# Four expert tiles of the MoE layer moved ahead of the final table, beside the last group's attention and router

## The reference

```python
h = tok(x)                                # softmax-weighted pairs: 256 -> 128 tokens each
h = h + rwkv_attn(layernorm(h))           # a linear recurrence along the tokens
h = h + ffn(layernorm(h))                 # 192 -> 768 -> 192, exact gelu
h = h + attn(layernorm(h))                # 12 heads, softmax over the queries, + its residual
# mixture of experts on flat = h, 8192 tokens, 8 experts, the top 2 of each token:
for e in range(8):
    w_e = sum(top_w * (top_i == e))       # the token's weight for expert e, 0 for most
    out = out + w_e * (gelu(flat @ w1[e] + b1[e]) @ w2[e] + b2[e])
return h + out
```

## Time and profile before

| | |
|---|---|
| median of 3 runs | 1794.03 us |
| the profiled execution | 1808.08 us, of it the span 1806.3 us |
| busy in the span | PE 1576.6 us (87%), DVE 1369.8 (76%), ACT 1192.0 (66%), POOL 739.9 (41%) |
| mean granted clock of TensorE | 0.912 of full |
| DMA | 145.41 MB, mean 81 GB/s |

### The profile page before, as it was taken

The page is one execution under the profiler, slowest core; times in us unless marked ns, Lnnn a source line. Parts: engine busy times, 40 slices in busy tenths (PEclk is TensorE's granted clock), DMA queues, the critical chain, the costliest instruction groups (busy, mean ns, idle before and its releaser), DMA issues.

```text
span 1806.3 us, 33908 instructions
## 1 busy us (share of the span) xinstructions
PE 1576.6 (87%) x10985; PEld 1269.9 (70%) x10985; DVE 1369.8 (76%) x2810; ACT 1192.0 (66%) x3269; POOL 739.9 (41%) x743
## 2 busy tenths in 40 slices
PE   3578999999999999999999887763999999999976
PEld 2255677677677677677677666543999999999876
DVE  4675788778788788778778743334899989999986
ACT  1245787877887787778778767543666666666643
POOL 0111142332332333333233232203577777777775
PEclk6798899989999899989989978656999999999988
DMA  4000010110110111011010000244677776677662
GB/s 118 26 27 17 20 51 28 43 51 26 41 50 31 36 50 38 30 50 44 24 50 30 22 34 25 99 148 146 168 169 167 172 160 159 160 166 171 159 152 64
DMA packets 121870, 145.41 MB, mean 81 GB/s; under 512 B 21074, under 2 KB 100419, under 8 KB 121795
## 3 DMA queue, kind: packets, MB, share of 16 engines
q1 hardware_dynamic: 92432, 113.00, 20.8%
q0 software_dynamic: 26592, 29.92, 8.9%
...
## 4 chain that ended last, share of the span: by engine, by line
PE 74%; DVE 9%; ACT 8%; issue 4%; SPq 2%; POOL 1%; DMA 1%; POOLq 0%; ACTq 0%; DVEq 0%
PE ps L934 12%; PE ps L947 9%; PE ps L716 7%; PE ps L791 5%; PE ps L702 5%; PE ps L949 4%; PE ps L807 4%; PE ps L597 3%; PE ps L708 3%; PE ps L556 3%; PE ps L737 3%; PE ps L820 2%; PE ps L749 2%; ACT probs L1091 2%; PE ps L603 2%
## 5 line engine op out<-in xcount | busy, mean ns | idle before, releaser
L1330 POOL DMA_INDIRECT out<-ey,etoken x142 | 253.9, 1788 | 143.6 <-DVE ey L1847 48.4
L1091 ACT ACTIVATE probs<-ps,nmax 128x128 f32<-128x128 f32 x768 | 272.2, 397 | 24.2 <-DVE nmax L1570 24.1
L947 PE MATMUL ps<-w_hl,h_hi 128*128 128x384 f32 x852 | 252.3, 366 | 12.3 <-DVE ey L1847 12.3
L1203 ACT ACTIVATE h_full<-ps,eb 128x512 f32<-128x512 f32 (+1 forms) x234 | 158.4, 677 | 154.0 <-PE ps L934 153.8
L1570 DVE TENSOR_REDUCE nmax<-ps 128x6 f32<-128x768 f32 x128 | 121.5, 953 | 134.1 <-PE ps L791 133.0
L949 PE MATMUL ps<-w_hl,h_lo 128*128 128x192 f32 x852 | 215.4, 253 | 0.0
L1091 ACT ACTIVATION_READ_ACCUMULATOR probs<-ps,nmax 128x1 f32 x768 | 182.1, 237 | 0.0
L1320 POOL TENSOR_TENSOR w_lo<-w_raw,w_hi 128x1536 fp32r<-128x1536 f32 x39 | 156.5, 4013 | 39.4 <-ACT w_hi L1183 39.4
L947 PEld LDWEIGHTS ps<-w_hl,h_hi 128*128 128x128 f32 x852 | 162.8, 191 | 13.7 <-issue 13.2
L949 PEld LDWEIGHTS ps<-w_hl,h_lo 128*128 128x128 f32 x852 | 165.3, 194 | 0.0
L1807 DVE TENSOR_TENSOR h_lo<-h_full,h_hi 128x512 fp32r<-128x512 f32 (+1 forms) x234 | 148.0, 686 | 16.7 <-ACT h_hi L1204 16.3
...
## 6 DMA issues: line engine op xcount, KB each, us to landing
...
ex<-expert_rows_in SPq DMA_DIRECT2D x32, 528.0 KB, 5.4
...
w_raw<-in_L_ffn_w SPq DMA_DIRECT2D x78, 192.0 KB, 5.7
...
expert_rows_in<-xt SPq DMA_DIRECT2D x17, 528.0 KB, 7.0
...
```

Source lines behind the costliest of these rows:

```text
L947: nc.tensor.matmul(ps[:, 4 + s, 0:2 * C], h_hi[b][:, m, q], w2_hl[b][:, m, :], start=(m == 0), stop=False)
L1091: last = nc.scalar.activation(probs[:, t % 2, HJ * c + j, :], ps[:, 4 + j, c * P:(c + 1) * P], ACT.Exp, bias=nmax[:, t, j, c:c + 1], accum ...
L1203: nc.scalar.activation(h_full[:, m, 0:n], ps[:, m % 4, 0:n], ACT.Gelu, bias=eb1[u][:, m:m + 1])
L1330: nc.gpsimd.indirect_dma_start(total, bass.IndirectOffsetOnAxis(ap=etoken[u][:, s:s + 1], axis=0), ey[b][:, s, :], None, bounds_check=NB * ...
```

## The change

The kernel after does the first four expert tiles (`EARLY = 4`) before the final table exists.

- When 15 of the 16 groups are counted, `first_tiles` (VectorE, right after `pad_rows`) finds the expert with the most tokens and the one with the second most. Tiles 0, 1 and 2 are the first three of the former, tile 3 is the first of the latter. It writes their entries of the table and sets `first_ready`.
- SP issues, behind the pad stores, the loads of tile 0 and tile 1, the rows of tiles 2 and 3, and the weights of tile 3. Tile 2 uses tile 0's weights, which stay in their buffer, so there is one load and one split fewer of w1 and of w2 (`splits`, `kept`).
- In round 18 the steps of tiles 0 and 1 stand between those of the last group's attention and router, on each engine. Tile 0's downward half, tile 2's and tile 3's steps stand around the final table.
- The final table has NU = 35 entries, of which NFU = 28 full; it takes away from the counts what the four tiles have taken, and adds to the row of an expert's tiles the rows that are done (`begun`). It has links for that (37 in all with those of `first_tiles`, 30 before).
- SP waits for the table and the last scatter only ahead of tile 4's rows.
- `e_down` waits for the second link of the previous result (`d_exp`), not for the last (`e_y`).
- Buffers are declared in another order, so that the first tiles' buffers lie over parts of the tower that are no longer used by then; the table's temporaries move from `hid` and `buf` to `probs`.
- The helpers of the expert steps are moved ahead of `round_` unchanged, but for the bank that tile 0's transposes use (`rows_bank`: 0, later 2) and the ranges of blocks that `e_gelu` and `e_low` take.

```diff
+    EARLY = 4
+    NFU, NU = NF - EARLY, NT - EARLY
...
+            kept = 1 if t[1] % HB == 0 and at_least(t, HB) else 0
+            return (LB // HB) * t[0] + t[1] // HB + 1 - kept
+
+        def splits(t, d=0):
+
+
+            n = number(t) + d
+            return n if not isinstance(t[0], int) or n >= HB else n + 1
 
         def at_least(t, n):
             return not isinstance(t[0], int) or number(t) >= n
+
+        def last_round(i):
+            return isinstance(i, int) and i == NG + 2
+
+        def early(j):
+
+
+            return (j // LB, j % LB)
+
+        def rows_bank(t):
+
+
+            return 2 if at_least(t, 1) else 0
...
-            sp.wait_ge(S["h_stored"], 16 * NG)
-            sp.wait_ge(S["scattered"], 16 * 2 * G * NG)
-            sp.wait_ge(S["table_ready"], 1)
...
-                    if not at_least(t, 1):
-                        load_weights(t)
-                        sp.wait_ge(S["pads_stored"], 16 * (2 * E + 1))
-                        load_rows(t)
...
+            sp.wait_ge(S["first_ready"], 1)
             sp.wait_ge(S["b1_stored"], 16)
-            expert_steps(sp, e_step, 0)
+            load_weights(early(0))
+            sp.wait_ge(S["scattered"], 16 * 2 * G * (NG - 1))
+            load_rows(early(0))
+            load_rows(early(1))
+            load_weights(early(1))
+            load_rows(early(2))
+            load_rows(early(3))
+            load_biases(early(2))
+            store_h(NG - 1)
+            load_weights(early(3))
+
+
+            sp.wait_ge(S["pads_stored"], 16 * (2 * E + 1))
+            sp.wait_ge(S["scattered"], 16 * 2 * G * NG)
+            sp.wait_ge(S["table_ready"], 1)
+            expert_steps(sp, e_step, EARLY)
...
+                    if m == 3 and not at_least(t, 1):
+                        pe.wait_ge(S["hF_ready"], G * NG)
...
+                if at_least(t, 1):
+                    pe.wait_ge(S["d_exp"], RESULT_LINKS * j)
+                else:
+                    pe.wait_ge(S["counted"], 1)
...
                 if gr is not None: c_project(gr, 1)
+                if last_round(i): e_transposes(early(0))
                 if gr is not None: c_values(gr, 2, gc)
...
+                if last_round(i): e_up(early(0))
                 if gr is not None: r_transposes(gr, gc)
+                if last_round(i): e_transposes(early(1))
...
                 if gb is not None: b_mlp_up(gb, 3)
+                if last_round(i): e_up(early(1))
                 if gr is not None: r_places(gr)
...
+            e_transposes(early(2))
             pe.wait_ge(S["slots_ready"], NG)
             counts(NG)
...
+            e_down(early(0))
...
-            expert_steps(pe, e_step, -2)
+            expert_steps(pe, e_step, 1)
...
                 if gr is not None: c_exps(gr, 1, 1)
+                if last_round(i): e_weights(early(0))
                 if gc is not None: ln_out(gc, "c", hnC, hC, rstdC, shiftC)
...
                 if gr is not None: c_values(gr, 1)
+                if last_round(i): e_weights(early(1))
                 if ga is not None: a_kv(ga, "k", k_s)
                 if gr is not None: c_exps(gr, 3, 0)
                 if gr is not None: c_exps(gr, 3, 1)
                 if gr is not None: c_values(gr, 2)
+                if last_round(i): e_rows(early(0))
                 if gc is not None: transposed(gc, "c", hTC, 4)
...
                 if gb is not None: transposed(gb, "b", hTB, 2)
+                if last_round(i): e_gelu(early(0), (0, 1))
                 if gr is not None: r_out(gr)
+                if last_round(i): e_gelu(early(0), (2, 3))
                 if gr is not None: transposed(gr, "r", hTC, 4)
+                if last_round(i): e_rows(early(1))
+                if last_round(i): e_gelu(early(0), (4, 5))
...
+            e_gelu(early(1))
+            e_rows(early(2))
+            e_weights(early(3))
+            e_gelu(early(2))
+            e_rows(early(3))
+            e_gelu(early(3))
+            e_weights(early(4))
+            e_rows(early(4))
...
-            expert_steps(act, e_step, -2)
+            expert_steps(act, e_step, 3)
...
+                if gs is not None: r_scatter(gs)
+                if last_round(i): e_weights(early(0))
+                if last_round(i): e_weights(early(1))
+
+            rounds(pool, round_)
...
-            pool.wait_ge(S["pads_stored"], 16 * (2 * E + 1))
-            expert_steps(pool, e_step, -2)
+            pool.wait_ge(S["h_stored"], 16 * NG)
+            expert_steps(pool, e_step, 1)
...
+            def first_tiles():
...
+                link = table.link
+                link(nc.vector.max(most_n[:, :], n_seen[:, :]))
+                link(nc.vector.max_index(most_i[:, :], most_n[:, :], n_seen[:, :]))
+                link(nc.vector.tensor_copy(most[:, :], most_i[:, 0:2]))
+                nc.vector.tensor_copy(expert_of[:, 0:3], most[:, 0:1].to_broadcast([P, 3]))
+                nc.vector.tensor_copy(expert_of[:, 3:4], most[:, 1:2])
+                nc.vector.tensor_scalar(most_off[:, 0:3], tile_i[0:1, 0:3], float(ET), None, ALU.mult)
+                nc.vector.memset(most_off[:, 3:4], 0.0)
+                nc.vector.tensor_tensor(taken[:, 0, :], lane8[:, 0, :], most[:, 0:1].to_broadcast([P, E]), ALU.is_equal)
+                link(nc.vector.tensor_tensor(taken[:, 1, :], lane8[:, 0, :], most[:, 1:2].to_broadcast([P, E]),
+                                             ALU.is_equal))
+                link(nc.vector.scalar_tensor_tensor(taken[:, 0, :], taken[:, 0, :], 3.0, taken[:, 1, :], ALU.mult, ALU.add))
+                nc.vector.tensor_copy(unit[:, :], tile_i[:, :])
+                nc.vector.tensor_copy(pair[:, :], pair_i[:, :, :].rearrange("p a b -> p (a b)"))
+                nc.vector.tensor_copy(odd[:, :], odd_i[:, :, :].rearrange("p a b -> p (a b)"))
+                nc.vector.memset(place_in[:, :], 0.0)
+                nc.vector.tensor_copy(tile_exp[:, 0:EARLY], expert_of[0:1, 0:EARLY])
+                nc.vector.scalar_tensor_tensor(tile_row[:, 0:EARLY], expert_of[0:1, 0:EARLY], float(REGION), most_off[:, :],
+                                               ALU.mult, ALU.add).then_inc(S["first_ready"], 1)
+                nc.vector.tensor_copy(mth[:, :, :], mth_i[:, :, :])
...
+                if isinstance(gs, int) and gs == NG - 1:
+                    e_low(early(0), (0, 1, 2, 3))
+                    e_rows(early(1))
                 if gs is not None: r_pick(gs)
+                if isinstance(gs, int) and gs == NG - 1:
+                    e_low(early(0), (4, 5))
+                    e_weights(early(1))
+                    for j in range(EARLY):
+                        e_pick(early(j))
...
+                if last_round(i): e_weights(early(0))
...
+                if last_round(i): e_rows(early(0))
                 if gr is not None: c_attn_add(gr, 3)
...
+            nc.vector.tensor_copy(n_tok[:, :], ps[:, 7, 0:E]).then_inc(S["counted"], 1)
+            e_rows(early(2))
+            e_low(early(1), (0, 1, 2))
+            dve.wait_ge(S["counted"], 1)
+            link(nc.vector.scalar_tensor_tensor(n_tok[:, :], taken[:, 0, :], float(-ET), n_tok[:, :], ALU.mult, ALU.add))
...
+            e_low(early(1), (3, 4, 5))
+            e_result(early(0))
+            link(nc.vector.tensor_tensor(passed[:, :, :], per(unit[:, :], 0, [P, NU, 2 * E]),
+                                         per(unit_end[:, :], 1, [P, NU, 2 * E]), ALU.is_ge))
             link(nc.vector.tensor_reduce(exp_f[:, :], passed[:, :, :], AX.X, ALU.add))
...
+            e_rows(early(3))
+            e_low(early(2))
             link(nc.vector.tensor_scalar(is_half[:, :], exp_f[:, :], float(E), float(E), ALU.is_ge, ALU.mult))
...
+            for n, tiles in ((0, 3.0), (1, 1.0)):
+                nc.vector.tensor_scalar(begun[:, n, :], exp_f[:, :], most[:, n:n + 1], tiles * ET, ALU.is_equal, ALU.mult)
+            nc.vector.tensor_scalar(expert_of[:, EARLY:NT], exp_f[:, :], float(E - 1), None, ALU.min)
...
+            for n in range(2):
+                link(nc.vector.tensor_tensor(off_f[:, :], off_f[:, :], begun[:, n, :], ALU.add))
+            link(nc.vector.tensor_copy(tile_row[:, EARLY:NT], off_f[0:1, :]))
             dve.sem_inc(S["table_ready"], 1)
...
+            e_result(early(1))
...
-            expert_steps(dve, e_step, -2)
+            expert_steps(dve, e_step, 2)
```

476 lines of the change are left out of this document (241 added, 235 removed).

## The result

The kernel after takes 1784.68 us as a median (1776.55 to 1793.74, 14 runs), the kernel before 1806.6 us (1791.66 to 1813.04, 14 runs, among them the three whose median is given ahead): ratio 0.9887, 95% interval 0.9862 to 0.9912. By the ratio that is 20.4 us less (15.9 to 24.9); the medians themselves lie 21.9 apart. Ratios leave out executions in a slower state (one of before, beside b0, e4, e5 and e6, took 2300.59 us at a granted clock of 0.625), and on the chip of a0, e1, e2 and e3 the executions of before and of three of these four spread over 31 to 53 us, which arises ahead of the seam (the kT copy starts at 1235.7 us in a0's trace and at 1200.2 to 1210.1 in the others), so that from there marks are read and not ratios.

A forecast was written before the change was run, and what follows sets the result against it. TensorE was taken to bound the expert loop but to idle at the seam before it. Places 25 us later, then 41.2 us less to tile 4, plus 2 for the clock: -14 from 1794, so 1780 us, range 1762 to 1795.

The forecast's parts named there:

- Step 1: Last group's attention: ScalarE waits for tile 0's w1 behind the pad stores, +15.0 us; smaller terms +2 and +1.5.
- Rival A: At ScalarE's first split: the first loads do not hold ScalarE, only the split's 1.5 us remains; 1766 us, chance 0.15.
- The two smaller terms: Last group's attention: tile 1's w1 split on ScalarE adds +2 us, GpSimd's w_lo splits blocking VectorE add +1.5.
- Step 2: Tiles 0 and 1's up-matmuls ahead of the router's places: tile 1's take 6.9 us, places come 25 us later.
- Step 3: TensorE beside the final table: 28.4 us of early tiles' work where it did nothing before, until 1272.4; the gain.
- Step 4: Final table lengthened by VectorE's tile work, ready at 1272.3; TensorE waits 7 us, tile 4's up-matmuls start at 1287.5.
- The clock: TensorE's granted clock around the early tiles: one or two falls during waits cost 2 us.
- Rival B: Tiles 0 to 3: TensorE's clock stays at 1.2 GHz, making the kernel 24 us slower, 1818 us; chance 0.09.
- Rival C: At the final table: its chain, delayed by VectorE and w_lo, takes the gain back; 1788 to 1792 us, chance 0.16.
- Step 5: The rest: omitted load and split 0, moved buffers 0, e_down's earlier release 0 to 2 us, not counted.

The follow-up runs named there:

- b0: The kernel before, unchanged, run again for its marks at the seam: 1801.53 us, one run.
- e4: Kernel after, loads untouched, but first tiles' splits and transposes moved behind attention or router work on four engines: 1773.36 us, ratio 0.9826 to before.
- e5: e1 plus, on VectorE, tile 3's row split and tile 2's low halves moved behind the table's last link: 1758.48 us, ratio 0.9741 to before.
- e6: Kernel after with only tile 3's row split and tile 2's low halves moved behind the table's last link on VectorE: 1775.62 us, ratio 0.9847 to before.
- a0: The kernel after, unchanged, run again on a slower chip: 1864.38 us, with before at 1881.36 us there.
- e1: Kernel after with tiles 0 and 1's weight loads issued ahead of the pad stores: 1831.01 us on a slower chip; repeated on the other chip 1765.25 us, ratio 0.9745.
- e2: Kernel after with eight more pad-sized stores, to rows nobody reads, between the pad stores and the first loads: 1849.84 us on the slower chip.
- e3: Kernel after with the down-matmuls waiting again for the previous result's last operation (e_y): 1865.35 us on the slower chip.
- e8: The kernel before with only its buffers declared in the order of the kernel after: 1800.40 us, ratio 0.9966 to before.
- e7: e5 with tile 3's row split back inside the table, only tile 2's low halves behind it: 1757.05 us, ratio 0.9716 to before.

## Why the prediction came out as it did

The forecast was 1780 us, with a range of 1762 to 1795, and the median is 1784.68. The seam was forecast at -14 and measured at -16 to -18. Two more things moved the total, in opposite directions: the base of 1794.03, a median of three runs, was low against the 1806.6 of 14 runs, and the buffers gave some 6 us. 17 + 6 = 23 against a measured 20.4 (15.9 to 24.9), if the order of the buffers acts in the kernel after as it does in e8, which no run shows. That the total came within 5 us of the forecast is in part luck: the base was 12.6 us too low, and the gain, some 6 to 8 us larger than the forecast 14, made up for half of it. The change is 1.1% faster, while the most likely class given was within 1%.

In what follows the marks of after are moved by 8.15 us (1162.72 - 1154.57), so that they stand beside the predicted times.

**Step 1 was right in its cause and its sum.** c_exps(15, 2, 0) was to start at 1197.0 and started at 1197.9 (1189.71 + 8.15), 15.9 us later than before against +15.0. (ScalarE's idle time, said to be some 15 us, is 17.5; for 2.5 of it ScalarE stood idle there before too.) The first w1 load was issued at 1180.95 and w1 was there 7.4 us later (6.7 forecast) because of the stores queued ahead. e2 shows it from the other side: 12.3 us more for 8 stores, 1.5 each, at the 1.6 us apart at which pads are issued. Rival A (the load overtakes, 1766) is out. The Trainium skill, "DMA: Bandwidth & Descriptors", section "Two DMAs through the same engine are not ordered", says that descriptors of one queue start in order; these runs agree. The two smaller terms came out otherwise than said. The exps of t = 3, before:

```profile
1189.57 0.37 ACT L1091 ACTIVATE probs<-ps,nmax 128x128 f32<-128x128 f32 x1 [2.15 <-DVE nmax L1570]
...
1192.73 0.37 ACT L1091 ACTIVATE probs<-ps,nmax 128x128 f32<-128x128 f32 x1 [0.96 <-DVE nmax L1570]
```

Their first half started 15.95 us later than that (1197.37 + 8.15), so tile 1's split added 0.1 us and not 2: its 2.35 us (0.87 waiting, 1.48) lie where ScalarE had waited 2.15 for the maxima. Their second half started 17.5 us later (1202.09 + 8.15), 1.6 more, behind GpSimd's w_lo, against +1.5. That w_lo blocked VectorE where forecast: the w2 copy took 3.75 us instead of 0.76, and a vpad multiply 2.82 instead of 0.36, and only the second lay on the path. The last projection ended at 1219.1 (1209.26 + 1.65 + 8.15), forecast 1219.9.

**Step 2 was right in sum, with two errors that cancel in part.** Tile 1's up-matmuls started at 1232.6 instead of 1234.1, but took 9.7 us instead of 6.9. The clock had fallen, which the step had not priced (stretches of after around them, columns as above, the granted clock third from the end):

```profile
1224.00:1228.00 4.00, 3.58 (x9) 2.84 (x10) 3.86 (x17) 1.86 (x5) 0.00 (x0) 0.50 0.00 0
1228.00:1234.00 6.00, 6.00 (x23) 4.72 (x21) 2.64 (x17) 4.60 (x9) 0.00 (x0) 0.81 0.34 98
```

The places came at 1242.25 (1241 forecast), 26.0 us later than before (+25), the counts at 1243.7 (1243.8).

**Step 3 was right.** TensorE was free for tile 4 at 1272.6 (1268.13 - 3.69 + 8.15); forecast 1272.4. This is the gain, and it arrived at tile 4's mark.

**Step 4: the table was right, the wait behind it too long.** The table was ready at 1271.7 (forecast 1272.3), although one of the three 0.96 us operations of tile 0's result took 3.85 us beside w_lo of tile 3; 2 us had been set aside for that. Tile 4's rows landed 3.4 us after their issue, and not 5.7 as I had taken from the w1 loads of the busy loop: TensorE waited 3.7 us instead of 7. Their issue in SP's queue:

```profile
1264.69 0.33 SPq L538 DMA_DIRECT2D ex<-expert_rows_in  x1
```

Of the 3.2 us saved, 2.1 were lost again (9.8 us from the transposes to tile 4's mark, forecast 7.7), as the transposes and the first down-matmuls ran at a low clock behind that wait:

```profile
1268.00:1272.00 4.00, 3.87 (x19) 3.87 (x20) 2.31 (x4) 0.00 (x0) 0.00 (x0) 0.59 0.90 207
```

Tile 4's mark came at 1286.05 (1287.5 forecast). e6 and e5 confirm that its place among the tiles' work delays the table by 5 us. At the mark that was worth 1 to 2 us in them, where tile 3's row split became late instead, and 4.6 in e7, where it did not.

**The clock** was sized too low: 2 us were added for one or two falls, and the two at 1224 and 1268 cost 2.8 (9.7 instead of 6.9) and 2.1. Both are inside the marks, which show -17.7 all the same, since tile 4's rows and other terms came out shorter than forecast. Rival B (24 us slower, TensorE stays at 1.2 GHz) is out: 0.81 and 1.00 were granted where it needed 0.50. Rival C (the table chain takes the gain back) is out: the wait at tile 4's rows was 3.7 us, its bound 15.

**Step 5 is the step that failed**, in two terms put at nothing. "The moved buffers change no instruction" is true, but e8 measures 6 us for them (2.4 to 9.9); through what is open. And e_down's earlier release (0 to 2 was said, not counted) saves 2 to 6 us of waiting by e3, of which between none and some 3 us reach the end. That nothing is lost behind tile 4's mark held.

What I did not see in advance is the size of what was left. Step 1 named the 15 us wait and its cause, and I took it as the price of the change; it was the price of a few lines' places. With the two weight loads ahead of the pads the same idea gains 2.5% instead of 1.1%.
